# A windowed-attention block on one core: the softmax exponentials and the layer-norm copies are put in another place on ScalarE

## The reference

```
qkv = shift_tokens(x) @ Wqkv;  q, k, v = split(qkv) into heads of 64
q = l2norm(q) * qs;  k = l2norm(k) * ks;  q, k = rotary(q, k)
sim = q_window @ [k_window_before, k_window].T * 8, masked
o = softmax(sim) @ [v_window_before, v_window]
x = x + o @ Wo
h = shift_tokens(x);  h = (h - mean) / sqrt(var + 1e-5) * g + b
a, gate = split(h @ W1 + b1)
x = x + (a * gelu(gate)) @ W2 + b2
```

## Time and profile before

| | |
|---|---|
| median of three runs | 5069.15 us |
| the profiled execution | 5069.15 us, its span 5066.9 us |
| PE busy | 4537.1 us, 90% of the span |
| DVE, ACT, POOL busy | 77%, 63%, 54% |
| L0 stage | about 719 to 3950 us |
| L1 stage | about 4160 to 5050 us |
| one pair in steady state | 32.5 us in L0, 24.5 us in L1 |

### The profile page before, as it was taken

How to read it: one execution, slowest core, us unless ns; L and a number is a source line. 1 busy time by engine, 2 the same in 40 slices (tenths; PEclk the granted TensorE clock), 3 DMA queues, 4 the chain that set the end, 5 groups by cost and what they waited for, 6 DMA issues and landing times. The chain is left out here.

```text
span 5066.9 us, 219416 instructions
## 1 busy us (share of the span) xinstructions
PE 4537.1 (90%) x81616; PEld 3412.1 (67%) x81616; DVE 3885.6 (77%) x8190; ACT 3172.1 (63%) x6718; POOL 2758.0 (54%) x3917
## 2 busy tenths in 40 slices
PE   4568948999999999999999999999998587999996
PEld 3556736777777777777777777777776454666665
DVE  6974567888888888888888888888885766777775
ACT  2003526777777777777777777777776445777775
POOL 0013116666666666666676666666664335555552
PEclk7987979999999999999999999999999788999998
DMA  2000125555555455555555555555553004444442
GB/s 77 1 1 23 42 60 132 144 138 139 144 136 145 134 146 133 151 132 151 132 150 136 148 133 149 135 147 135 149 135 99 11 13 109 116 111 114 114 113 76
DMA packets 704922, 564.39 MB, mean 111 GB/s; under 512 B 223492, under 2 KB 629864, under 8 KB 704008
## 3 DMA queue, kind: packets, MB, share of 16 engines
q1 hardware_dynamic: 691080, 537.36, 40.0%
q10 hardware_dynamic: 13312, 22.02, 1.4%
HBM read 359.38 MB, written 200.02 MB: 110 GB/s over the span
## 5 line engine op out<-in xcount | busy, mean ns | idle before, releaser
L2154 POOL TENSOR_TENSOR L_qk<-L_cos_part,L_sin_part 128x512 f32<-128x512 f32 x896 | 1129.7, 1275 | 94.0 <-DVE L_sin_part L2031 93.0
L1815 ACT ACTIVATE L_squares<-L_ps_q 128x512 f32<-128x512 f32 x896 | 535.1, 597 | 817.6 <-PE L_ps_q L1541 811.5
L1541 PE MATMUL L_ps_q<-L_w_qkv,L_xT 128*128 128x512 f32 x1792 | 981.1, 630 | 14.5 <-DVE L_sin_part L2031 10.1
L2145 POOL TENSOR_TENSOR L_qk<-L_qk,L_rnorm 128x1024 f32<-128x1024 f32 (+1 forms) x512 | 865.1, 1690 | 18.2 <-POOL L_rnorm L2128 1.1
L1577 PEld LDWEIGHTS L_ps_t<-L_ident,L_qk 128*128 128x128 f32 x3584 | 447.5, 141 | 481.0 <-issue 381.7
L2030 DVE TENSOR_TENSOR L_cos_part<-L_ps_q,L_rot 128x512 f32<-128x512 f32 x896 | 610.5, 681 | 39.8 <-POOL L_rot L2164 31.1
L2031 DVE TENSOR_TENSOR L_sin_part<-L_ps_q,L_rot 128x512 f32<-128x512 f32 x896 | 610.1, 681 | 0.0
L2032 DVE TENSOR_REDUCE L_sumsq<-L_squares 128x8 f32<-128x512 f32 x896 | 605.8, 676 | 0.0
L2122 POOL TENSOR_TENSOR L_nw_a<-L_rnorm 128x32 f32<-128x32 f32 (+1 forms) x256 | 59.9, 234 | 911.6 <-ACT L_rnorm L1845 911.6
L1577 PE MATMUL L_ps_t<-L_ident,L_qk 128*128 128x128 f32 x3584 | 540.6, 274 | 6.5 <-DVE z L2095 3.9
L1826 ACT ACTIVATE L_qkT<-L_ps_t 128x512 f32<-128x512 f32 x896 | 530.1, 592 | 14.5 <-PE L_ps_t L1577 14.4
(11 more groups left out here) (293 smaller groups left out, 8948.4 us busy)
## 6 DMA issues: line engine op xcount, KB each, us to landing
L_val<-v_rows SPq DMA_DIRECT2D x896, 260.0 KB, 3.9
v_rows<-L_val SPq DMA_DIRECT2D x384, 260.0 KB, 2.1
v_rows<-L_val SPq DMA_DIRECT2D x512, 65.0 KB, 2.0
L_rot_base<-in_rot SPq DMA_DIRECT2D x256, 128.0 KB
v_rows<-L_val SPq DMA_DIRECT2D x128, 130.0 KB, 2.1
L_x_in<-x_rows SPq DMA_DIRECT2D x512, 32.0 KB
mid_rows<-z SPq DMA_DIRECT2D x256, 64.0 KB, 1.6
L_f_in<-mid_rows SPq DMA_DIRECT2D x256, 64.0 KB, 2.0
```

The source lines that it names most:

```text
L1541: nc.tensor.matmul(ps_q[j % 2][:, :], xT[:, parity(t), :], w_qkv[:, 0:2, 256 * j:256 * j + 256], start=True, stop=True).then_inc(S["proj_p ...
L1815: nc.scalar.activation(squares[:, j % 2, :], ps_q[j % 2][:, :], ACT.Square).then_inc(S["sq_done"], 1)
L2145: nc.gpsimd.tensor_tensor(v, v, r, ALU.mult).then_inc(S["normed"], 1)
L2154: nc.gpsimd.tensor_tensor(qk[:, t % 2, h, s, :], cos_part[:, j % 2, :], sin_part[:, j % 2, :], ALU.add).then_inc(S["added"], 1)
```

## The change

Only the ACT `emit` of `local_block_stage` changes. In hf 0 of an even tile the exponentials go from behind the second table load to ahead of the first; with `NS == 1` (L1) the copy of the transposed probabilities goes ahead of the first table load too, behind the exponentials. In the three other halves the exponentials and the copy change places. In hf 1 of an even tile `normalised`, which stood at the end behind `input_copy`, comes right behind `val_copy`, ahead of both.

```
                     if hf == 0 and T % 2 == TO_UP % 2:
+                        exponentials(k, T, hf)
+                        if NS == 1:
+                            prob_copy(k, T, hf)
                         if live(k, T - TO_UP):
                             nc.scalar.preload_act_table_set("gelu_and_others")
-                        prob_copy(k, T, hf)
+                        if NS == 2:
+                            prob_copy(k, T, hf)
                         gates(k, T)
                         val_copy(k, T, hf)
                         if live(k, T - TO_UP):
                             nc.scalar.preload_act_table_set("natural_log_exp_and_others")
-                        exponentials(k, T, hf)
                     else:
                         val_copy(k, T, hf)
+                        if hf == 1 and T % 2 == TO_LN % 2:
+                            normalised(k, T)
+                        exponentials(k, T, hf)
                         prob_copy(k, T, hf)
-                        exponentials(k, T, hf)
                     if hf == 1:
                         input_copy(k, T)
-                        if T % 2 == TO_LN % 2:
-                            normalised(k, T)
                     else:
                         previous_keys(k, T)
```

## The result

The changed kernel takes 5227.34 us, median of four runs (5225.71 to 5236.42); the kernel before, run beside it, 5066.0 (5061.91 to 5071.28). The ratio is 1.0321, with a 95% interval from 1.0308 to 1.0334. It is slower, by the mechanism forecast, but by 161 us instead of 120, and that is 7 us outside the range (5140 to 5220). The profiled execution took 5233.22 us.

A forecast was written before the change was run, and what follows sets the result against it. PE was taken to bound both stages, so added waits are paid in full. L0 terms 48.4 and 28.2 us plus L1 terms 23.5 and 20.1 make 120 us on 5069, taken as 5190 us; range 5140 to 5220.

The forecast's parts named there:

- The gate term: Even tile, hf 0: later gelu table load delays gates and PE, 0.52 us a pair in L0, 0.81 in L1.
- no slack anywhere: L0, hf 0 of even tiles: no slack between ACT's gelu table load and PE's out transposes, by way of `att`.
- The layer-norm copies and the exponential ahead of the copy: Even tile, hf 1: later copy of the probabilities delays PE's scores, 0.30 us a pair in L0, 0.67 in L1.
- X: Start of ACT's value copy in hf 1 of the even tile, L0; PE's scores forecast at X + 2.51, before X + 2.22.
- PE starts 0.15 later as behind `att`: L0, hf 1 of even tiles: PE's scores start 0.15 us after the copy of the probabilities ends.
- the sum of the upper bounds: All terms at their upper bounds (0.63, 0.50, 0.9, 0.9): 159 us more, 5228.
- The other halves: Odd tile, hf 0 and hf 1: copy slips 0.5 us into existing room, nothing charged; if room were missing, 15 us in L0.
- L1: Second stage: 29 x 0.81 = 23.5 us for gates and 30 x 0.67 = 20.1 for hf 1; pair from 24.5 to 26.0.
- Only the gates count: Rival: in hf 1 the copy of the probabilities still makes it ahead of the scores; 72 us, 5141; chance 0.12.
- no change: Rival: the added delay falls in time in which PE has other work; 5069 us; chance 0.04.
- faster: Rival: earlier layer-norm copies remove PE's waits for them, 8.9 us in all; 5060 us; chance 0.03.
- the granted clock: Rival: new PE waits let the clock fall to 1.2 GHz in part of L1's pairs, adding 80 us, 5270; chance 0.05.

The follow-up runs named there:

- e8_between_rotations: Against the kernel before: DVE's deviations moved to hf 1, in L0 between the rotations with related steps reordered; in L1 `gated` starts at its first gate; 5013.65 us, ratio 0.9905.
- e4_wait_last: Against the changed kernel: in PE's scores the wait for the probabilities' copy stands last of the waits instead of first; 5191.03 us, ratio 1.0244 to the kernel before.
- e3_swap_only: Against the kernel before: exponentials and copy of the probabilities change places in the three halves without gates, layer-norm copies stay at the end; 5078.4 us, ratio 1.0031.

## Why the prediction was right in kind and wrong in size

- *PE is the bound, and what makes it wait is paid.* Right: PE's work per pair is unchanged, its idle time in L0 went from 0.4 to 1.4 us.
- *The gate term, 0.52 in L0 and 0.81 in L1.* Right: +0.51 and +0.79 in the kernel that has this part alone, 45.7 and 22.0 us where 48.4 and 23.5 were forecast. How it shows was not quite as said: in L0 PE's wait for `att` is 0.33 in the pair, not 0.75, since the same delay meets PE one step earlier, at the weighted values: 0.39 of it there by the starts, 0.12 at `att`. In the kernel before, those had about 0.1 us to spare, so "no slack anywhere" was right for the chain by way of `att`, not for this one. The kernel before also does not have every pair alike, as I wrote: most take 32.5 us, but one in each pass takes about 34.
- *The layer-norm copies and the exponential ahead of the copy.* ACT's side was right to 0.01 us: first layer-norm copy at X + 0.50, exponential at X + 1.26 (forecast 1.27), copy at X + 1.78 (1.77). **The step that failed is the next one: "PE starts 0.15 later as behind `att`".** It was 0.54. With 0.54 the same sum gives X + 2.91, and 0.69 a pair instead of 0.30; the part alone measured 0.67. Over 94 pairs the difference is 94 x 0.37 = 35 us, of the 38 by which L0 was missed. The 0.15 was read at `out_transposes`, which has no further steps between its wait and its first matmul. At the scores there are four. That the steps are the cause is shown by the kernel with the wait put last: 0.10 us in place of 0.54 and 0.40 a pair back.
- *The bounds of that term.* I gave 0.15 and 0.50 and varied only ACT's overlap and a latency of nothing; the latency was not varied upwards, though it was taken from another instruction. With 0.69 for the upper bound the sum of the upper bounds would have been 5246. As it stood that sum was 5228, but I gave the range only up to 5220, without a reason. That 5228 is next to the result is luck: it puts too much on the gates and on L1, and too little on this term.
- *The other halves: nothing is charged.* Right for nearly all pairs, and by less room than thought: of the 1.13 us by which the copy came early, 0.54 is needed by PE's sequencer and 0.5 taken by the slip. The exchange alone costs 9 to 10 us, round the layer changes, where ACT issues weight loads. In the whole change it shows in the same pairs, above all in the second of the two, which takes 34.2 us and not 33.7. Over L0 those pairs make about 8 us; other uneven pairs and the end of the stage lost less than the term says, so the total hides it.
- *L1.* The total came out right (44.8 against 43.6) with offsetting errors. A steady pair went from 24.52 to 26.26, +1.74, not +1.48. Of the 0.26 too little, 0.25 is the same latency: 0.40 from the end of the copy (4652.20) to the scores (4652.60), with three further steps on the sequencer. But of the pairs that already took longer, most stayed or nearly so (26.39 before, 26.36 after), and so gave part back, while one in each of two passes lost more (28.13 to 31.12, 27.94 to 31.57). Why those have room, or less of it, I did not follow up. The longer refinement wait (0.30 of ACT for POOL) came about as worked out.
- *The rivals.* "Only the gates count", "no change" and "faster" are excluded by the interval, and the granted clock was 1.00 in L0 and 0.99 over L1 in both kernels. PE's waits of 1.40 us in the steady pairs of L1 did not move it. The Trainium skill ("TensorE: Matmul & The Clock Gate", Part 1) says that idling lowers the clock. The trace agrees at the changes of layer in L1, where the granted clock falls behind a wait of 3.46 us before the change and of 3.28 after it. Behind the new waits it fell once (after 1.83 us, near the end of L1), and the time at 1.2 GHz is the same in all.

What is not shown: whether the sequencer steps would cost the same if they were of another kind. Only the place of one wait was changed, not the number of steps.

## What to carry to other kernels

A margin between two engines is not the time from the end of the one's work to the start of the other's: from it goes what the waiting engine still has to do behind its wait, and this is read at that very instruction, not at another. Put the wait that comes last in time last in the code, and the cheap ones ahead of it. When work is moved out of one stall, look for who waits on the buffer of the work that it is put in front of; in `e8_between_rotations`, between two steps of which only the first is waited for, it brought no new wait of PE.

## What the runs showed of the hardware that was not expected

- Waits and register steps that have nothing to wait for still take about 0.1 us each on PE's sequencer when they stand behind a wait that has just been released. From the end of ACT's copy to the first matmul it was 0.54 us with five records on the sequencer between the two, the released wait's own among them (L0, hf 1), 0.40 with three (L1), 0.10 with none (`e4_wait_last`). There the other steps had run between 2187.29 and 2187.58, while PE was busy until 2188.93, and cost nothing.
- A DMA issued by ACT took 0.40 us of its sequencer, with 0.54 us of idle time between its activations around it (`e3_swap_only`, 2027.93); that shows in the time only where the room is already used up.
- Two delays of ACT that alone cost 9 and 17 us in L0 cost 66 together, since both draw on one margin of about 0.6 us.
